# Between attention and expert mixture: a pipeline by batch, and a gather of each tile in place of a scatter

## The reference, cut to what matters

```python
x = x + attn_out                              # attn_out = heads @ Wo + bo
nx2 = _layernorm(x, ln2_w, ln2_b)
gate_logits = nx2 @ gate_W                    # 8 logits a token
topk_vals, topk_idx = top_k(gate_logits, 2)
gate_w = softmax(topk_vals)
for e in range(8):
    h = gelu(nx2 @ fc1_w[e].T + fc1_b[e])     # 256 -> 1024
    y = h @ fc2_w[e].T + fc2_b[e]             # 1024 -> 256
    moe_out += y * dense_gates[..., e]
return x + moe_out
```

## Time and profile before

| | us |
|---|---|
| median of 3 runs | 2034.35 |
| profiled execution | 2036.74 |
| its span, first to last instruction | 2035.0 |
| last attention output written (DVE, L1535) | at 658.5 |
| first expert matmul starts (PE, L954) | at 780.8 |
| last scatter issued (POOL, L595) | at 774.7 |
| last expert output evacuated (DVE, L1645) | at 1075.2 |
| last gather of the outputs issued (POOL, L602) | at 1117.0 |

### The profile page before, as it was taken

The page is one execution under the profiler, slowest core; times in us unless marked ns, Lnnn a source line. Parts: engine busy times, 40 slices in busy tenths (PEclk is TensorE's granted clock), DMA queues, the critical chain, the costliest instruction groups (busy, mean ns, idle before and its releaser), DMA issues.

```text
span 2035.0 us, 31702 instructions
## 1 busy us (share of the span) xinstructions
PE 1750.3 (86%) x10850; PEld 1061.0 (52%) x10851; DVE 1119.4 (55%) x2984; ACT 839.9 (41%) x2048; POOL 205.9 (10%) x282
## 2 busy tenths in 40 slices
PE   4999997777887756999991799999999999977998
PEld 2555554333333546999990244444444444356886
DVE  3777777456663351222223576666655765747775
ACT  2888885425554302333340254444443543520000
POOL 0111111201111241000006200000000000020000
PEclk8999999769998757999996699999999999977999
DMA  7788884200001721111116000000000000020001
GB/s 268 247 282 281 289 297 163 72 1 1 1 1 38 256 96 55 36 36 36 36 31 222 3 0 1 1 1 1 1 1 0 1 1 1 0 83 1 0 0 41
DMA packets 63704, 146.64 MB, mean 72 GB/s; under 512 B 6360, under 2 KB 41312, under 8 KB 58976
## 3 DMA queue, kind: packets, MB, share of 16 engines
q1 hardware_dynamic: 60512, 136.69, 19.6%
q0 software_dynamic: 3072, 8.39, 1.2%
HBM read 86.34 MB, written 58.72 MB: 71 GB/s over the span
## 4 chain that ended last, share of the span: by engine, by line
PE 78%; ACT 7%; DVE 6%; issue 4%; POOL 3%; DMA 1%; SPq 0%; DVEq 0%; ACTq 0%; POOLq 0%
PE PS L623 14%; PE PS L1096 9%; PE PS L954 7%; PE PS L939 7%; PE PS L1023 6%; PE PS L1033 6%; PE PS L1048 5%; PE PS L821 5%; PE PS L698 4%; PE PS L720 3%; PE PS L1011 3%; PE PS L731 2%; PE PS L839 2%; POOL YP L602 2%; POOL pair_tokens L595 1%
## 5 line engine op out<-in xcount | busy, mean ns | idle before, releaser
L1316 ACT ACTIVATE P<-PS,nm 128x512 f32<-128x512 f32 x256 | 173.8, 684 | 321.1 <-DVE nm L1707 321.1
L1707 DVE TENSOR_REDUCE nm<-PS 128x2 f32<-128x1024 f32 x128 | 156.7, 1225 | 107.3 <-PE PS L1023 107.3
L1033 PEld LDWEIGHTS PS<-idf,P 128*128 128x128 f32 x1024 | 109.7, 141 | 104.6 <-issue 104.6
L1519 DVE CUSTOM_DVE_ANT_0 dump<-PS,maskw 128x256 f32<-128x256 f32 (+3 forms) x256 | 114.9, 487 | 87.1 <-PE PS L826 81.5
L1450 DVE CUSTOM_DVE_ANT_0 SN<-PS,SR 128x128 f32<-128x128 f32 (+3 forms) x256 | 115.3, 488 | 75.4 <-PE PS L702 75.0
L954 PEld LDWEIGHTS PS<-xT,W1c 128*128 128x128 f32 x1280 | 151.1, 194 | 4.4 <-ACT xT L1277 2.4
L954 PE MATMUL PS<-xT,W1c 128*128 128x128 f32 x1280 | 151.7, 277 | 1.8 <-ACT xT L1277 1.8
L821 PE MATMUL PS<-QP,KP 32*128 32x128 f32 (+3 forms) x512 | 111.3, 508 | 45.0 <-ACT PTf L1242 38.4
L1023 PE MATMUL PS<-K,Q 64*128 64x512 f32 x512 | 145.5, 645 | 0.9 <-DVE Q L1695 0.9
L939 PE MATMUL PS<-EW,hT 128*128 x640 | 145.0, 379 | 0.9 <-DVE ysb L1645 0.9
L1033 PE MATMUL PS<-idf,P 128*128 128x128 f32 x1024 | 139.2, 279 | 6.6 <-ACT PTb L1325 6.6
(11 more groups left out here) (219 smaller groups left out, 3054.4 us busy)
## 6 DMA issues: line engine op xcount, KB each, us to landing
SR<-rel SPq DMA_DIRECT2D x16, 1024.0 KB, 8.0
rel<-EN SPq DMA_DIRECT2D x15, 1024.0 KB, 4.8
SR<-rel SPq DMA_DIRECT2D x16, 768.0 KB, 6.4
rel<-EN SPq DMA_DIRECT2D x15, 768.0 KB, 4.2
SR<-rel SPq DMA_DIRECT2D x16, 512.0 KB, 4.6
EW<-in_fc1T SPq DMA_DIRECT2D x8, 1024.0 KB, 12.1
EW<-in_fc2T SPq DMA_DIRECT2D x8, 1024.0 KB, 11.9
rel<-EN SPq DMA_DIRECT2D x15, 512.0 KB, 2.9
```

What stands on the lines that cost most here:

```text
L1033: last = nc.tensor.transpose(TR1[j][:, c * P:c * P + P], P1[s % 4][:, j, c * P:c * P + P], idf[:])
L1316: last = af(P1[s % 4][:, j, :], PD[s % 2][:, j, :], ACT.Exp, bias=nm1[:, s % 4, j:j + 1], accum_out=sm1[:, s % 4, j:j + 1])
L1707: v.tensor_reduce(nm1[:, s % 4, :], PD[s % 2][:], AX.X, ALU.max, negate=True).then_inc(c_max, 1)
```

## The change

The handover is rewritten in three ways.

**By batch.** The stages run as steps n = 0 to 6, and in step n PE does, in this order: transposes of `ON` for batch n, the product with `WO` for batch n-1, transposes of `NM` for batch n-2, gate logits for batch n-3, counts for batch n-4. Work passes through four PSUM banks (0 to 3, `T_USES`), whose order of uses is fixed over all steps. A transposed half batch fills one bank (128x512) and is evacuated by one instruction; for `NM` the first half by ACT, the second by DVE. The product with `WO` takes two blocks to a bank. The counts are accumulated in bank 4, which a product with zeros (`none`) clears in step 1.

**A table from slots to tokens.** For each slot number, `above` marks the tiles that begin below it, `low` is its place within the tile, `picks` is a one-hot row of that place, and `marks` holds the token's partition and block number. Thirty-two bfloat16 products picks x marks, one for each choice and block, sum into bank 5, and the difference of neighbouring columns gives `inv`: for every slot, its token's number. A slot that no token has gets token 0. `NM` is stored as it is (`tokens_normalised`, 4 stores by SP), and before every tile POOL gathers its 128 rows with one indirect DMA, which waits for the transposes of the tile two before. The 32 scatters and the 10 clearing stores are gone.

**Moved or dropped.** The bias `fc2b` is broadcast to all partitions (1 MB) and added when a tile's output is evacuated, in place of the products of step 8 above. `B1t` is dropped: DVE reads the expert's bias by the expert's number. The softmax of the gates and `gpair` move behind the last tile. The constants are loaded before the expert weights. `NT0` is 39 in place of 40, the most tiles that 4096 slots over 8 experts can fill. Expert 4 waits for the transposes of `ON`, then SP stores `NM` batch by batch, loads `fc2b`, expert 3 and expert 5.

```diff
-NT0 = TOP0 * T // P + E0
+NT0 = TOP0 * T // P + E0 - 1
...
+T_USES = []
+for _n in range(B + 3):
+    T_USES += [("t", _n, _k) for _k in range(DK) if _n < B]
+    T_USES += [("w", 2 * (_n - 1) + _i) for _i in range(2) if 0 <= _n - 1 < B]
+    T_USES += [("i",)] * (_n == 1)
+    T_USES += [("n", _n - 2, _k) for _k in range(DK) if 0 <= _n - 2 < B]
+    T_USES += [("g", _n - 3)] * (_n >= 3)
...
+        def t_free(eng, use):
+            i = T_AT[use]
+            if i >= NTB:
+                eng.wait_ge(t_r[i % NTB], i // NTB)
+            return PS[i % NTB]
...
@@ SP @@
-            for i in range(NT0 // 4):
-                sp.dma_start(xs.rearrange("(t p) d -> p t d", p=P)[:, 4 * i:4 * i + 4], zero[:]).then_inc(s_xz, 16)
...
-            wait_all_stored(sp, "ont")
+            t_done(sp, ("t", B - 1, DK - 1))
             expert_weights(4)
...
+            for b in range(B):
+                if b == B - 1:
+                    t_done(sp, ("w", 2 * B - 1))
+                    sp.dma_start(fc2b[:], A["fc2b"].rearrange("e d -> (e d)").partition_broadcast(P)).then_inc(ld["fc2b"], 16)
+                sp.wait_ge(ln_sem[2]["nrm"], RT * b + RT)
+                sp.dma_start(xs.rearrange("(t p) d -> p t d", p=P)[:, RT * b:RT * b + RT], NM[:, RT * b:RT * b + RT])\
+                    .then_inc(s_nm, 16)
             sp.wait_ge(s_xh, TB)
...
-            wait_stored(sp, "rt0", 0)
+            t_done(sp, ("g", B - 1))
             expert_weights(5)
...
@@ POOL @@
-            for tb in range(TB):
-                for i in range(TOP0):
-                    pool.indirect_dma_start(xs, bass.IndirectOffsetOnAxis(pos[i][:, tb:tb + 1], 0), NM[:, tb, :],
-                                            None).then_inc(s_xs, 16)
+            pool.wait_ge(s_nm, 16 * B)
+            pool.wait_ge(s_inv, 3)
+            for j in range(NT0):
+                if j >= 2:
+                    pool.wait_ge(s_e["xt"], j - 1)
+                pool.indirect_dma_start(xin[j % 2][:], None, xs, bass.IndirectOffsetOnAxis(inv[:, j:j + 1], 0))\
+                    .then_inc(s_xin[j % 2], 16)
...
@@ PE @@
+            for n in range(B + 3):
+                for k in range(DK):
+                    if n < B:
+                        attended_t(n, k)
+                for i in (2 * n - 2, 2 * n - 1):
+                    if 0 <= i < 2 * B:
+                        out_projection_t(i)
+                if n == 1:
+                    counts_t()
+                for k in range(DK):
+                    if 0 <= n - 2 < B:
+                        normalised_t(n - 2, k)
+                if n >= 3:
+                    gate_t(n - 3)
+                if n >= 4:
+                    ranks_t(n - 4)
+            ranks_t(B - 1)
+            for g in range(TOP0 * TB):
+                i, tb = divmod(g, TB)
+                pe.wait_ge(s_pick, g + 1)
+                mm(PS[5][:, 0:2 * NT0], picks[:, g % 8, :], marks[:, i, tb].rearrange("p c j -> p (c j)"), start=(g == 0),
+                   stop=(g == TOP0 * TB - 1)).then_inc(s_used, 1)
...
@@ ACT @@
+            for n in range(B + 2):
+                for k in range(DK):
+                    if n < B:
+                        attended_t(n, k)
+                if 0 <= n - 1 < B:
+                    sqrt_t(n - 1)
+                if 0 <= n - 2 < B:
+                    normalised_t(n - 2)
...
@@ DVE @@
+            for n in range(1, B + 3):
+                if n <= B:
+                    out_projection_t(2 * n - 2)
+                    out_projection_t(2 * n - 1)
+                    stats_t(n - 1)
+                if n == 1:
+                    counts_t()
+                if 0 <= n - 2 < B:
+                    normalised_t(n - 2)
+                if n <= B:
+                    normalise_t(n - 1)
+                if n >= 3:
+                    two_largest_t(n - 3)
...
             for i in range(TOP0):
+                link(v.tensor_tensor(above[:, i], pos_f[i][:].unsqueeze(2).to_broadcast([P, TB, NT0]),
+                                     thr[:].unsqueeze(1).to_broadcast([P, TB, NT0]), ALU.is_gt))
+                link(v.tensor_reduce(high[:], above[:, i], AX.X, ALU.add))
+                link(v.scalar_tensor_tensor(low[i][:], high[:], -float(P), pos_f[i][:], ALU.mult, ALU.add))
+                v.tensor_scalar(low[i][:], low[i][:], float(P - 1), None, ALU.add)
+                v.tensor_scalar(marks[:, i, :, 0, :], above[:, i], idcol[:, 0:1], None, ALU.mult)
+                link(v.tensor_tensor(marks[:, i, :, 1, :], above[:, i],
+                                     jtab[:, 0:TB].unsqueeze(2).to_broadcast([P, TB, NT0]), ALU.mult))
+                for tb in range(TB):
+                    g = i * TB + tb
+                    if g >= 8:
+                        dve.wait_ge(s_used, g - 7)
+                    v.tensor_scalar(picks[:, g % 8, :], iota[:], low[i][:, tb:tb + 1], None, ALU.is_equal).then_inc(s_pick, 1)
...
+            dve.wait_ge(s_used, TOP0 * TB)
+            v.memset(inv_f[:, NT0:], 0.0).then_inc(s_inv, 1)
+            v.tensor_copy(inv_t[:], PS[5][:, 0:NT0]).then_inc(s_inv, 1)
+            dve.wait_ge(s_inv, 2)
+            link(v.scalar_tensor_tensor(inv_f[:, 0:NT0], PS[5][:, NT0:2 * NT0], float(P), inv_t[:], ALU.mult, ALU.add))
+            v.tensor_tensor(inv[:], inv_f[:, 0:NT0], inv_f[:, 1:NT0 + 1], ALU.subtract).then_inc(s_inv, 1)
...
             def outputs(j, s, stored):
+                bias = fc2b[:, bass.ds(dve.value_load(te[0:1, bass.ds(j, 1)]) * D, D)]
...
-                v.tensor_copy(ysb[s][:], PS[5][:, 0:D]).then_inc(s_e["ys"], 1)
+                v.tensor_tensor(ysb[s][:], PS[5][:, 0:D], bias, ALU.add).then_inc(s_e["ys"], 1)
...
                 v.tensor_copy(W1c[s][:], EW[:, bass.ds(e, 1), 0:DK * F0].rearrange("p e f -> p (e f)")).then_inc(s_e["w"], 1)
+                b1 = B1[:, :, bass.ds(dve.value_load(te[0:1, bass.ds(j, 1)]), 1)].rearrange("p f e -> p (f e)")
```

More of the change, by code:

```diff
@@ L58 @@
 M_W = {use: i for i, use in enumerate([_u for _u in M_USES if _u[0] != "p"])}
+T_USES = []
[5 more added lines that the diff above has]
+    T_USES += [("g", _n - 3)] * (_n >= 3)
+T_USES += [("g", B - 1)] * (("g", B - 1) not in T_USES)
+T_AT = {use: i for i, use in enumerate(T_USES)}
+NTB = 4
 def head_of(g, j):
@@ L208, in build @@
         B1 = place("B1", [P, FK, E0], F32)
-        B1t = place("B1t", [P, NT0, FK], F32, rPT + 32 * KB)
         b1c = [place(f"b1c{i}", [P, FK], F32) for i in range(2)]
@@ L248, in build @@
         GW = place("GW", [P, DK, E0], F32)
-        fc2b = place("fc2b", [E0, D], F32)
         rb_row = place("rb_row", [P, E1], F32)
@@ L889, in _ @@
-            ln_transposes(2, "ln2", lambda tb: NM[:, tb])
-            pe.wait_ge(ld["late"], 80)
-            wait_all_stored(pe, "ln2")
-            bank = bank_for_write(pe, "rt0", 0)
-            for tb in range(TB):
-                for k in range(DK):
-                    last = mm(bank[:, tb * E0:tb * E0 + E0], NT[:, k, tb * P:tb * P + P], GW[:, k, :],
-                              start=(k == 0), stop=(k == DK - 1), skip_group_check=True)
-            wrote(last, "rt0", 0)
-            pe.wait_ge(ld["route"], 32)
@@ new lines, in normalised_t, with gate_t @@
+            def normalised_t(b, k):
+                bank = t_free(pe, ("n", b, k))
+                pe.wait_ge(ln_sem[2]["nrm"], RT * b + RT)
+                for q in range(RT):
+                    last = nc.tensor.transpose(bank[:, q * P:q * P + P], NM[:, b * RT + q, k * P:k * P + P], idf[:])
+                last.then_inc(t_write(("n", b, k)), 1)
+            def gate_t(b):
+                bank = t_free(pe, ("g", b))
+                for k in range(DK):
+                    t_done(pe, ("n", b, k))
+                for q in range(RT):
+                    t = slice((b * RT + q) * P, (b * RT + q + 1) * P)
+                    for k in range(DK):
+                        last = mm(bank[:, q * E0:q * E0 + E0], NT[:, k, t], GW[:, k, :], start=(k == 0), stop=(k == DK - 1),
+                                  skip_group_check=True)
+                last.then_inc(t_write(("g", b)), 1)
@@ new lines, in two_largest_t @@
+            def two_largest_t(b):
+                t = slice(RT * b, RT * b + RT)
+                bank = t_written(dve, ("g", b))
+                v.tensor_copy(lg[:, t, 0:E0], bank[:, 0:RT * E0].rearrange("p (t e) -> p t e", e=E0))\
+                    .then_inc(t_read(("g", b)), 1)
+                t_done(dve, ("g", b))
+                for tb in range(RT * b, RT * b + RT):
+                    last = v.max(top[:, tb, :], lg[:, tb, 0:E0 + 8])
+                link(last)
+                link(v.memset(top[:, t, TOP0:8], LOW))
+                for tb in range(RT * b, RT * b + RT):
+                    last = v.match_replace(lg2[:, tb, 0:E0 + 8], top[:, tb, :], lg[:, tb, 0:E0 + 8], LOW)
+                link(last)
+                v.tensor_tensor(msk[:, t, :], lg2[:, t, 0:E0], lg[:, t, 0:E0], ALU.not_equal).then_inc(s_rt["mask"], 1)
```

302 lines of the change are left out of this document (162 added, 140 removed).

## The result

| us | before | after |
|---|---|---|
| median of the runs | 2036.79 (4 runs) | 1979.76 (4 runs) |
| ratio | | 0.9722 [0.9669, 0.9774] |
| measured again later | 2033.38 (11 runs) | 1978.88 (5 runs), 0.9739 [0.9718, 0.9759] |
| span of the profiled execution | 2035.0 | 1975.2 |
| last attention output to counts read | 71.8 | 46.8 |

The forecast was 1978 with a range of 1962 to 2006. The last 3.4 are not shown to be an effect of the change: in the fourteen executions profiled for this study this stretch is 955.0 to 956.3 in five and 957.7 to 959.3 in nine, and code that is the same has both (955.9 and 957.7). The second measurement of the changed kernel was expected to read its counts 46 to 48.5 us after the last attention output; in its profile it was 48.9.

The account below looks back on a forecast made before the run. No single engine was taken to bound the handover (a relay, a quarter of it POOL's scatter); PE bounds the tiles. Handover 50.5 plus tile 7.2 off 2036.74 gave 1979.0, stated as 1978 because the median is lower; range 1962 to 2006.

Parts of the forecast that it names:

- the three terms (3.7, 13, 2.5): Counts read to 724: slot arithmetic 3.7, DVE's table passes for both choices 13, tiles' experts and `inv` 2.5; total 19 us.
- The walk through the routing: Step-by-step sum of PE and DVE work and waits from 658.2 to counts read, taken as 705.
- PE then waits for `none`: Steps 0 and 1: after the first products at 664, PE waits for DVE's zero record until 667.
- 1.6 us lost: Step 3: products wait for a bank that ACT empties only after batch 1's root; 1.6 us, to 681.
- from here I take half clock: After the last `WO` products at 689, transposes 1.8, gates 3.5, counts 2.2, then gates and counts again, at half clock.
- the second term: Last part of the routing, at half clock: from batch 3 normalised at 690.3 to counts read at 705.
- Full clock to the end gives 699: End of the routing: with no half clock after the last `WO` products, counts are read at 699, not 705.
- The signs named: Trace checks: right if DVE over 80% busy 663 to 700, clock 1.00 to 688; wrong if 0.50 before 680.
- DVE being nearly full: Step 4 of the routing: reason given for batch 3 being normalised only at 690.3.
- the first rival: Half clock all through the routing: PE takes 68 us, counts read at 728, 23 later; 2001 us; chance 14%.
- Three batches are in flight: Routing: the argument given against PE and DVE alternating within a step.
- no overlap: Routing: four banks and ordered engines make PE and DVE alternate, 34 + 28 and some 4 of hops; 1997 us; 8%.

Follow-up runs that it names:

- e12_fill: Changed kernel with earlier zero record, reordered ScalarE/VectorE steps, later expert list, 11 unused products behind the table, 20 more in the routing: 1966.14 us, 0.9648.
- e11: Changed kernel with stages in serial order, small moves out of the banks, and three whole-stage waits of the kernel before put back: 1998.1 us, 0.9815.
- e3_serial: Changed kernel with each handover stage run over all four batches before the next; wide moves and signals by batch kept: 1988.89 us, 0.9764.
- e9_serial_narrow: Changed kernel with stages in serial order and moves out of the banks in small pieces (128 or 256 columns); signals by batch kept: 1989.03 us, 0.9787.
- e8_copy_later: Changed kernel with VectorE's 1.23 us copy of the first expert's up weights waiting until the first gather has landed: 1981.51 us, 0.9722.

## Why the prediction was right, and where only its sum was

**The path and the two big terms.** First expert matmul at 729.74, said 730.3. Counts read at 705.67, said 705; `inv` begun at 723.5, said 724; table 17.8 where 19 was said. In the table, the three terms (3.7, 13, 2.5) came out at 3.6, 12.5 and 1.8. Both replacements were measured alone: the scatter put back costs 26 of the stretch, three of the whole-stage waits 12 of the 25.

**The walk through the routing had two errors that cancelled, in this execution.** "PE then waits for `none`" was right, 2.45 us, and the bank wait of "1.6 us lost" was 1.96. But a pause cost more than itself: behind each, the clock fell (it was 0.50 from 667.5 to 670.9 and from 677.8 to 681.1), and the products took 4.94 and 5.41 in place of 3.7, so 1.2 and 1.7 more. The second is the firmer of the two: in the five other executions with this order the products behind the first pause took 3.6 to 3.9, those behind the second 5.4 in four and 3.7 in one. These two are most of the 3.9 by which batch 3's normalised tokens came late (694.2, said 690.3). On the other side, "from here I take half clock" was too dark for this profile: the clock held at 1.00 until 698.2, through the transposes, the gates of one batch and its counts. From batch 3 normalised to counts read, 11.4 in place of 14.7.

That the end point was hit to 0.7 us (705.67, said 705) is therefore luck. In the four other executions whose clock fell about the last pause, the second term is as forecast, 14.6 to 15.1, and the routing takes 48.5 to 48.9, where the walk, 705 less 658.5, has 46.5. The walk is 2.0 to 2.4 us short there, and most of that lies before batch 3 is normalised.

**"Full clock to the end gives 699"** is not borne out by e12_fill, though that read its counts at 699.2: the walk's 699 has the two waits in it, and e12_fill has neither, but 20 products more and half clock from 696.4.

**The signs named.** First matmul, counts, table, gathers and 39 tiles of 7.25 came as said. Two signs of being right did not: DVE was busy for 25.3 of the 37 us between 663 and 700, 68% and not over 80%, so "DVE being nearly full" holds only from 682 to 694 (11.1 of 12 us); and the clock was not at 1.00 to 688. One sign of being wrong did come, a clock of 0.50 before 680, for 3.4 us and again from 677.8; it cost some 3 us and not the 23 of the first rival. From the last gather of the outputs to the end it is 913.6 us and before 916.7 (the last gather before starts at 1118.3, not at 1117.0), a difference in the spread named above.

**"Three batches are in flight" was believed for the wrong reason.** The 25 us were put down to the order by batch. The same stages in serial order, with signals by batch and wide moves, keep 20 of them. What the old kernel lost was a wait for a whole stage at each border, where PE stood still for 7.7 and 6.8 us and DVE for 13.8. The rival "no overlap", priced at 34 + 28 = 62 us plus hops, mistook order for overlap; the run nearest to it is e11, at 68.6.

**The clock's rule.** With transposes alone PE kept 1.00 for 1.91 us at 658.3 and for 3.7 us in e3_serial, and steps with few products kept it too. In this profile the clock fell three times: behind a pause under transposes (667.5), behind a pause under `WO` products (677.8), and at 698.2 after 4 us of transposes, gates and counts without a pause. The first rival did not come true. Nor did transposes keep a fallen clock down. In e3_serial PE does nothing but transposes from 693.81 to 698.27, the clock is 0.50 at their start and 1.00 from 698.2, and the next 12 take 0.13 us each where the 20 before took 0.22:

```profile
693.81 4.45 PE L943 MATMUL PS<-idf,NM 128*128 128x128 f32 x20 [1.03 <-DVE NM L1652]
698.96 1.53 PE L943 MATMUL PS<-idf,NM 128*128 128x128 f32 x12 [0.69 <-DVE NT L1658]
```

```profile
692.00:696.00 4.00, 2.97 (x13) 2.68 (x14) 3.89 (x15) 0.94 (x2) 0.00 (x0) 0.50 1.09 371
696.00:700.00 4.00, 3.31 (x21) 2.95 (x20) 3.93 (x11) 1.56 (x2) 0.00 (x0) 0.74 1.06 367
```

In e9_serial_narrow (transposes alone from 687.30) and e11_whole_stages (from 686.02) the clock is likewise 1.00 from 691 on. The Trainium skill (TensorE: Matmul & The Clock Gate, Part 4: PE-mode transpose) says that full clock does not engage for transposes. These three traces do not agree, and the measurement decides. In the 8 us at half clock of the earlier trace rows, by contrast, its timeline has a pause of 0.2 us behind every four transposes; what kept the clock down there is not shown.

**The gather beside DVE.** The first gather took 1.49 us in place of 0.94 and those of the loop were hidden; e8_copy_later shows the copy as the cause of 0.39 of that. The Trainium skill (SBUF — State Buffer, Who interferes with whom) says that such a copy blocks GpSimd for the whole instruction, and the trace agrees: each gather that met a copy ended after it. The "up to 1.2 later" that the prediction drew from it was a bound that the first gather did not reach: 0.39 on POOL, 0.6 in landing.

**The tile.** 7.25 us, said and measured; but first up matmul to last output shrank by 5.3 only, and that the total still came out 2.1 below the sum (59.8 less, said 57.7) is owed to the 3.4 behind the last tile, which lie within the spread. The first tile's products took 6.70 at half clock where 5.92 had been (0.8; in the second profile of the changed kernel they took 5.27, and the same stretch shrank by 6.7), and the last two evacuations came 0.4 to 0.8 later behind their products. The new evacuation, which adds `fc2b` by the expert's number, was costed at nothing for DVE's low load. In the loop that holds; at the end nothing covers it.

**POOL's additions** did not meet the normalising (0.408 in the mean, has 0.81), and no product waited for an expert's weights: both as costed.

## What to carry to other kernels

Before rewriting an order, look at the waits at a stage's border: a signal for each batch in place of one for the whole stage gave half of the routing's gain here, and the order by batch 2.5 to 6.5 of 25 us. Where TensorE is near the path, a pause can cost more than itself through the clock behind it (here 1.7 us more behind a pause of 1.96, in five executions of six); move the small thing that it waits for ahead, or fill the pause with products that nobody reads. When two terms of a walk are uncertain and of opposite sign, a hit on the end point says nothing about either: check the walk at a point in between, and in a second execution.

## What the runs showed of the hardware

- TensorE was busy with gate products (128x128 stationary, 8 columns moving) without a pause, and the clock still fell: in e3_serial it was 1.00 from 700 to 704 and 0.61 from 704 to 708, with PE busy for all of it.

```profile
700.00:704.00 4.00, 4.00 (x39) 4.00 (x37) 2.81 (x18) 0.78 (x1) 0.00 (x0) 1.00 1.09 377
704.00:708.00 4.00, 4.00 (x25) 4.00 (x24) 2.94 (x30) 0.00 (x0) 0.00 (x0) 0.61 1.04 405
708.00:712.00 4.00, 4.00 (x21) 4.00 (x20) 1.67 (x16) 0.00 (x0) 0.00 (x0) 0.50 1.05 406
```

- In e12_fill, with 4 products of 128 columns between its groups of gates and counts and a 2 us pause filled with 8, it was 1.00 from 682 to 696.4.
- About the pause of 1.0 to 2.0 us before the last batch's transposes, the clock fell in seven of the nine executions in order by batch that leave it open: under the counts ahead of it in three, within it in two, under the transposes behind it in two. It held in two, one of which has the same code as one in which it fell.
- Transposes alone brought the clock from 0.50 to 1.00 in three executions (e3_serial at 698.2, e9_serial_narrow and e11_whole_stages by 691).
- A gather on GpSimd takes 0.94 us, 1.41 to 1.98 if a 1.23 us copy of VectorE falls on it. In the loop TensorE never waited for a gather.
